# Score products of three attention layers on 64 rows instead of 32, with one operand masked, and a new order of TensorE's steps

## The chip, the core and the metric

The program runs on one core of a Trainium2 chip, in one launch. Its time is the device time in microseconds (us), the median of three runs. The engines are TensorE (PE; PEld is its weight load), VectorE (DVE), ScalarE (ACT), GpSimd (POOL) and SyncE (SP), which issues the DMAs.

## What is computed

Four residual attention layers follow each other on `x` of shape (2, 128, 32, 32), that is two batches of 128 channels and N = 1024 places.

```python
# layer 0: 4 heads of 4 channels; softmax over the query index n
q, k, v = (einsum('hdc,bcn->bhdn', W, xf) + b for W, b in ...)
A = softmax(einsum('bhdn,bhdm->bhnm', q, k), axis=-2)
x = gamma * (Wo @ einsum('bhdn,bhnm->bhdm', v, A) + bo) + x
# layer 1: one head, q and k of 16 channels, v of 128
x = x + gamma * (v @ softmax(q.T k, axis=2))
# layer 2: 8 heads of 16 channels; group norm; k and v from the 2x2-pooled x (256 places)
attn = softmax(einsum('bhdq,bhdk->bhqk', q, k) * scale, axis=-1)
x = x + wproj @ (attn v)
# layer 3: group norm, one head of 128 channels
x = x + out_w @ softmax(q k.T * scale) v + out_b
```

All data are float32; some products are made from values rounded to `fp32r`.

## The kernel before

**Tiles and steps.** The work is cut into steps, and `ORDER` is a string with one letter for each step, in the order in which TensorE issues them. Every other engine walks the same list (`plan`) and does its part of each step, so the string sets the order of all queues. The letters: `N` projections and norms (`k`, `q`, `stats`, `norm`), `V` value projections, `A` and `B` score tiles, `T` the transpose of the maxima (`top`), `P` the product of probabilities and values, `E` and `Y` outputs, denominators (`den`), their broadcast (`bcast`) and projections of the output.

**A unit of attention** (layer L, batch b, group g) goes: eight A tiles (L784 for layers 0 and 1, L789 for odd tiles of some, L797 for layer 2, L802 for layer 3) make rounded scores of 128 x 1024 in `products`; DVE reduces each to its maxima (`neg_max`, L604, L601, L607). A transpose (L815) and one ACT copy turn the maxima into rows (`max_rows`), and DMAs from SP (L388, L393, L397, L399) put them beside an operand as one more row, so that the second product comes out with the maximum already taken off. Then eight B tiles (L823 in layer 0, L828 in layer 1, L834 in layer 2, L838 and L844 in layer 3) make the scores again with that row, ACT takes the exponent (L495) into a ring of `NP` = 8 tiles `probs`, and P steps multiply with the values into `attn_acc` (L863: four products, each 32 columns wide, side by side, in layers 0 and 2; L869: 128 columns in layers 1 and 3).

**Rings.** `products` has three slots of 128 x 1024 (`RING`); a slot is free when DVE (A, N steps) or ACT (B steps) has read it. A unit of layer 1 or 3 has its exponents summed on POOL and DVE (L366).

**Rows.** In layers 0 to 2 a head's operands stand in one of four groups of 32 partitions (`GROUP`). A score tile is two products, each with 32 rows of contraction, on two neighbouring groups: a head pair in layers 0 and 2, two halves of the columns in layer 1. Layer 0 has head pair `g // 2`; in layers 1 and 2 the pair of groups changes from tile to tile. This is the core of it in layer 0:

```python
rows = slice(GROUP * (2 * (g // 2) + a), GROUP * (2 * (g // 2) + a) + GROUP)
tile = slice(HALF * mh + 128 * mt, HALF * mh + 128 * (mt + 1))
mm = nc.tensor.matmul(slot(s)[:, halves[a]], RA[b][rows, tile], RB[b][rows, halves[nh]],
                      start=True, stop=True)
```

**A start** has the projections of batch 0 (L756 and L760, first and second half), for which ACT makes the rounded part (L456, `stage_hi`) and DVE the rest (L570). `RA` (`rounded_a`) holds k and `RB` (`rounded_b`) q of layer 0. `wait_tile` waits until a tile is complete, `wait_read` until it has been read.

Of the kernel before, what the change touches and what calls it, by code (L numbers as in the profile page):

```python
# [20 lines left out]
F32 = mybir.dt.float32  # L21
# [14 lines left out]
GROUP = 32  # L36
ONE = 16
RING = 3
MAX_DMAS = {0: 2, 1: 4, 2: 4, 3: 1}
NP = 8  # L40
# [7 lines left out]
FIRST = [("w0k", 128), ("b0k", 1), ("s0k", 1), ("w0q", 128), ("b0q", 1), ("s0q", 1), ("w0v", 16), ("b0v", 16)]  # L48
REST = [("gam0", 4), ("gam0c", 1), ("b0o", 1), ("w0o", 128), ("ident", 128), ("pick0", 72), ("w1q", 128), ("w1k", 128), ("b1q", 1),
# [25 lines left out]
def groups(L, b):  # L75
# [12 lines left out]
    "NNAAAAAAANNAVATAAABABABAABVBAPTAABPAABBABAABPBABPT"  # L88
    "ABAPABAPBABPBABABAPTBPPABBPABBPBBAPBBAPAPABPBABBPT"
    "AAVPPPBAEAEBABEBABPNNVABABBPTAAAPPPABABABABABBPTBA"  # L90
    "BAPAPABPPBABPAPPBAPPAPBABPPAPBAPATPBPPAPABPAAPEPBB"
    "BEBBTNPBBNPPBPNBPBNNBBBBPBVPPAAPAAPAAAAEATEABEBBBA"
    "AANNAVABABBPTABAAPBABABAPBAPPABBPBBETPPPPEBEBYEPBE"
    "PPPNBNPPBPNNBPPAAPABPAPPBAPPAAEPAPEVNTNBNPNNBBPBAA"
    "PAVAAPAAPAPPATAAPPABABABABABPTBBBPBBBPBPPBBBPPBEPP"
    "PEEYEENBNBBNNBAAPAAPPAPAAAPVPTPPBBBPBEPBPBEPPPPPBP"
    "PBPPPPPPEPPE"
# [28 lines left out]
def build_plan():  # L126
# [17 lines left out]
    following = {c: iter(s) for c, s in steps.items()}  # L144
    return [next(following[c]) for c in ORDER]


def attention_layers(nc, x, first, rest, sel, out):
# [61 lines left out]
    with ExitStack() as ctx:  # L210
# [22 lines left out]
        KF2 = [sb(f"k2_rows{b}", [128, 2, NKV]) for b in range(B)]  # L233
        KR2 = [sb(f"k2_rounded{b}", [128, 2, NKV], F32R) for b in range(B)]
# [32 lines left out]

        ps = ctx.enter_context(nc.psum_tensor("products", [128, RING, N], F32))
# [4 lines left out]
        cleared = sem("cleared")  # L273
        consts_ready, consts_act = sem("consts_ready"), sem("consts_act")
# [5 lines left out]
        act_copy = sem("act_copy")  # L280
        max_folded = sem("max_folded")
# [70 lines left out]

        norm_no = number(("norm",))
# [17 lines left out]
        def _(sp):  # L371
# [6 lines left out]
            for s in plan:  # L378
                kind, L, b = s[0], s[1], s[2] if len(s) > 2 else None
                if kind == "top":  # L380
# [4 lines left out]
                    if L == 0:  # L385
                        for a in range(2):
                            row = GROUP * (2 * (g // 2) + a) + ONE
                            sp.dma_start(RA[b][row:row + 1, halves[g % 2]].bitcast(F32),  # L388
                                         ZR[4 * a:4 * a + 4, i, :]).then_inc(maxrows_in[b], 16)
                    elif L == 1:  # L390
                        for j in range(4):
                            row, h = GROUP * j + ONE, j % 2
                            sp.dma_start(FA[b][row:row + 1, halves[h]], ZR[4 * h:4 * h + 4, i, :]).then_inc(maxrows_in[b], 16)  # L393
                    elif L == 2:
                        for j in range(4):
# [29 lines left out]
        def _(act):  # L425
            for s in plan:
# [9 lines left out]
                elif kind in ("q", "k"):  # L436

                    if s not in full_no:
                        wait_tile(act, s)
                        wait_ops_free(act, L, b)  # L440
                        nc.scalar.activation(KR2[b][:, :, :].rearrange("p g n -> p (g n)"), slot(s)[:, 0:2 * NKV],
                                             ACT.Identity, bias=w("one2k")).then_inc(act_copy, 1)
                        continue
                    for h in halves:
# [18 lines left out]
                        hi.then_inc(act_copy if h.start else act_half, 1)  # L463
                elif kind == "v" and L > 0:
# [31 lines left out]
                elif kind == "out" and (L in (0, 2) or s[3] == 0):  # L496
# [8 lines left out]
                    h = halves[s[3] % 2] if L == 0 else slice(0, N)  # L505
                    nc.scalar.activation(O[o_tile[u]][:, h], acc[:, h], ACT.Identity).then_inc(acc_out, 1)  # L506
# [534 lines left out]
```

## Time and profile before

| | us (the clock: share) |
|---|---|
| median of 3 runs | 434.34 |
| lowest and highest | 433.93, 436.12 |
| the profiled execution | 433.25 |
| its span, first to last instruction | 431.2 |
| mean granted clock of TensorE in the span | 0.865 |

The profile is of one execution. Its span is 2.05 us shorter than that execution's own time, and that time is 1.09 us under the median. The profile names idle time by what ended it, and it gives TensorE's granted clock by stretch, where 1.00 stands for 2.4 GHz and 0.50 for 1.2 GHz; the first 10.8 us have no clock record, and the page shows them as if at 1.00. TensorE's busy time is modelled from starts, so that a lone product counts with its latency.

### The profile page before, as it was taken

What the parts mean: (1) busy time and instruction counts of PE and PEld (TensorE: products, weight loads), DVE (VectorE), ACT (ScalarE), POOL (GpSimd) and SP (SyncE); (2) the same over time, 40 slices, a digit from 0 to 9 for tenths busy, and PEclk for the clock granted to TensorE, in tenths of its full rate; (3) what the DMA queues carried; (4) which work ended last, traced back from release to release, by engine and by line L of the source; (5) the groups of instructions that cost most, each with busy time, mean ns of one, the idle gap of its engine ahead of it and who ended that gap; (6) DMA issues with size and microseconds to landing.
All of it is one profiled execution on the core that took longest, in us unless ns stands there. A gap on an engine that the chain in (4) does not pass through costs nothing.

```text
span 431.2 us, 4565 instructions
## 1 busy us (share of the span) xinstructions
PE 375.4 (87%) x1756; PEld 162.1 (38%) x1756; DVE 252.0 (58%) x312; ACT 187.2 (43%) x228; POOL 53.3 (12%) x36
## 2 busy tenths in 40 slices
PE   5689789999899989877998898987988997899994
PEld 2245222334223342333442342453444233364541
DVE  1876776775845575383666345695296016592733
ACT  3034478856533357902365534215404571513210
POOL 4000000000006400000000043200420000300820
PEclk9685699988869985976599998988995899999998
DMA  7000000000000000000000000000000000000011
GB/s 277 0 0 2 0 1 3 0 2 0 2 1 2 0 0 0 3 0 3 0 1 2 2 0 0 0 0 2 1 3 1 2 2 0 0 2 0 2 49 49
DMA packets 1508, 4.44 MB, mean 10 GB/s; under 512 B 352, under 2 KB 720, under 8 KB 1360
## 3 DMA queue, kind: packets, MB, share of 16 engines
q1 hardware_dynamic: 1488, 4.16, 2.6%
q8 instruction: 14, 0.23, 0.2%
q14 instruction: 6, 0.05, 0.0%
HBM read 2.99 MB, written 1.05 MB: 9 GB/s over the span
## 4 chain that ended last, share of the span: by engine, by line
PE 65%; DVE 19%; ACT 5%; issue 5%; DMA 3%; SPq 2%; ACTq 0%; DVEq 0%
PE attn_acc L869 12%; PE attn_acc L863 9%; DVE neg_max L604 7%; PE products L834 6%; PE products L756 5%; PE products L838 5%; PE products L760 4%; PE products L823 3%; PE products L828 3%; PE products L768 3%; PE products L784 3%; DVE neg_max L601 3%; ACT probs L495 3%; PE products L898 2%; DVE neg_max L607 2%
## 5 line engine op out<-in xcount | busy, mean ns | idle before, releaser
L495 ACT ACTIVATE probs<-products 128x1024 f32<-128x1024 f32 x128 | 127.1, 1023 | 111.5 <-PE products L828 32.0
L604 DVE TENSOR_REDUCE neg_max<-products 128x2 f32<-128x1024 f32 x64 | 76.2, 1220 | 32.6 <-PE products L784 28.3
L869 PE MATMUL attn_acc<-probs,v 128*128 128x512 f32 x128 | 64.0, 612 | 0.0
L863 PE MATMUL attn_acc<-probs,v 128*32 128x512 f32 x384 | 59.6, 713 | 0.0
L601 DVE TENSOR_REDUCE neg_max<-products 128x4 f32<-128x1024 f32 x32 | 37.4, 1217 | 19.4 <-PE products L797 19.3
L366 POOL TENSOR_TENSOR prob_sum<-prob_sum,probs 128x1024 f32<-128x1024 f32 x16 | 38.5, 2405 | 72.7 <-ACT probs L495 71.6
L366 POOL TENSOR_TENSOR prob_sum<-probs 128x1024 f32<-128x1024 f32 x4 | 9.4, 2356 | 286.2 <-ACT probs L495 262.0
L607 DVE TENSOR_REDUCE neg_max<-products 128x1 f32<-128x1024 f32 x32 | 37.4, 1218 | 11.7 <-PE products L789 4.9
L784 PE MATMUL products<-rounded_b,rounded_a 32*128 32x512 f32 x128 | 35.3, 567 | 9.4 <-DVE neg_max L604 5.7
L823 PE MATMUL products<-rounded_a,rounded_b 32*128 32x512 f32 x128 | 34.6, 566 | 7.4 <-DVE neg_max L604 1.9
L838 PE MATMUL products<-rows_a,rows_b 128*128 128x512 f32 x64 | 31.9, 623 | 0.0
L869 PEld LDWEIGHTS attn_acc<-probs,v 128*128 128x128 f32 x128 | 22.0, 189 | 21.9 <-issue 18.0
L622 DVE RECIPROCAL recips<-products 128x128 f32<-128x128 f32 x10 | 9.5, 954 | 33.4 <-PE products L889 33.4
L784 PEld LDWEIGHTS products<-rounded_b,rounded_a 32*128 32x128 f32 x128 | 13.4, 211 | 33.4 <-DVE neg_max L604 15.9
L823 PEld LDWEIGHTS products<-rounded_a,rounded_b 32*128 32x128 f32 x128 | 13.5, 215 | 28.8 <-DVE neg_max L604 11.3
L834 PE MATMUL products<-rows_a,k_rows 32*128 32x512 f32 x64 | 20.5, 938 | 3.9 <-DMA rows_a<-max_rows 3.9
L506 ACT ACTIVATE attn_out<-attn_acc 128x512 f32<-128x512 f32 (+1 forms) x16 | 13.0, 811 | 23.0 <-PE attn_acc L869 13.8
L756 PE MATMUL products<-x,w 128*128 128x512 f32 x16 | 14.8, 1028 | 5.1 <-DMA x<-x 4.8
L863 PEld LDWEIGHTS attn_acc<-probs,v 128*32 128x32 f32 x384 | 9.1, 118 | 22.2 <-issue 17.3
L838 PEld LDWEIGHTS products<-rows_a,rows_b 128*128 128x128 f32 x64 | 12.5, 198 | 13.0 <-issue 12.3
L828 PE MATMUL products<-rows_a,rows_b 32*128 32x512 f32 x64 | 16.3, 639 | 0.6 <-DMA rows_a<-max_rows 0.6
L844 PE MATMUL products<-max_rows,max_picker 128*128 128x512 f32 x32 | 16.8, 605 | 0.0
(124 smaller groups left out, 390.1 us busy)
## 6 DMA issues: line engine op xcount, KB each, us to landing
w<-w_rest SPq DMA_DIRECT2D x1, 1235.0 KB, 7.9
x<-x SPq DMA_DIRECT2D x2, 512.0 KB, 4.4
y<-x SPq DMA_DIRECT2D x2, 512.0 KB, 2.6
tmp<-row_selector SPq DMA_DIRECT2D x1, 512.0 KB, 8.7
rounded_a<-max_rows SPq DMA_DIRECT2D x16, 2.0 KB
w<-w_first SPq DMA_DIRECT2D x1, 146.0 KB, 2.2
rows_a<-max_rows SPq DMA_DIRECT2D x8, 2.0 KB
rows_a<-max_rows SPq DMA_DIRECT2D x8, 4.0 KB
```

The lines of the kernel that those rows point to most:

```text
L366: engine.tensor_tensor(DS[:, :], first_in, P[:, n % NP, :], ALU.add).then_inc(den_acc, 1)
L495: nc.scalar.activation(P[:, n % NP, :], slot(s), ACT.Exp, scale=SCALE[L]).then_inc(read_act, 1)
L601: nc.vector.tensor_reduce(out=m2, in_=slot(s).rearrange("p (a i k) -> p a i k", a=2, i=2), op=ALU.max, axis=AX.X, negate=True).then_inc(re ...
L604: nc.vector.tensor_reduce(out=m[:, 2 * t:2 * t + 2], in_=slot(s).rearrange("p (a n) -> p a n", a=2), op=ALU.max, axis=AX.X, negate=True).t ...
L607: nc.vector.tensor_reduce(out=m[:, t:t + 1], in_=slot(s), op=ALU.max, axis=AX.X, negate=True).then_inc(read_dve, 1)
L756: nc.tensor.matmul(slot(s)[:, halves[0]], wt, src[:, halves[0]], start=True, stop=True).then_inc(half_full, 1)
L784: mm = nc.tensor.matmul(slot(s)[:, halves[a]], RA[b][rows, tile], RB[b][rows, halves[nh]], start=True, stop=True)
L823: mm = nc.tensor.matmul(slot(s)[:, halves[a]], RB[b][rows, 128 * t:128 * (t + 1)], RA[b][rows, halves[g % 2]], start=True, stop=True)
L834: mm = nc.tensor.matmul(slot(s)[:, halves[a]], KF2[b][rows, g, 128 * kt:128 * (kt + 1)], (FA, FB)[g][b][rows, halves[half]], start=True, s ...
L838: nc.tensor.matmul(slot(s)[:, h], FB[b][:, 128 * t:128 * (t + 1)], FA[b][:, h], start=True, stop=False)
L863: mm = nc.tensor.matmul(acc[32 * j:32 * j + 32, h], lhs, P[:, b_no[q] % NP, halves[a]], start=t0 == 0 if L == 0 else t0 % 2 == 0, stop=t0 ...
L869: mm = nc.tensor.matmul(acc[:, h], V13[b][:, t0, :], P[:, b_no[q] % NP, h], start=t0 == first, stop=t0 == last)
```

## The change

**Rows.** A group of 64 partitions (`WIDE`) takes the place of the two groups of 32. A score tile is still two products of 512 columns (four of 256 in layer 2's A), but each now has 64 rows of contraction: rows 0 to 63 and rows 64 to 127. In layers 0 and 2 the 64 rows hold two heads, one of each head pair, in 32 rows each; one operand exists in two copies, and in each the rows of the other head pair are zero, so that only one head is summed. For layer 0 the copies of q are `Q0` (`q_even`, pair 0) and `RB` itself (pair 1), made by ACT from `RB` with a scale of 1 or 0 for each partition (`group_mask`). For layer 2 `KR2` and `KF2` get two copies, by a second ACT and a second DVE instruction. Layer 1 has its 17 rows in 64, the rest being zero in the weights. The weights on the host are packed to match.

**DMAs of the maxima.** One for each unit of layers 0 and 2 (two and four before), two for layer 1 (four before). A DMA of layer 0 for pair 1 waits until the B tiles of pair 0 are made, as both pairs now use the same partitions of `RA`.

**Start.** DVE clears a tile `zeros`, and TensorE runs five products of 256 columns with it (`WARMUP`) before its first step.

**Ring.** `NP` goes from 8 to 13 `probs` tiles.

**Order.** `ORDER` has the same 462 letters in another order (the letter `W`, for which the code is there, does not occur).

```diff
-NP = 8
+NP = 13
+WARMUP = 5
...
                     if L == 0:
-                        for a in range(2):
-                            row = GROUP * (2 * (g // 2) + a) + ONE
-                            sp.dma_start(RA[b][row:row + 1, halves[g % 2]].bitcast(F32),
-                                         ZR[4 * a:4 * a + 4, i, :]).then_inc(maxrows_in[b], 16)
+                        row = GROUP * (g // 2) + ONE
+                        if g >= 2:
+                            wait_tile(sp, ("B", 0, b, g - 2, 7))
+                        sp.dma_start(RA[b][row:row + WIDE + 1:WIDE, halves[g % 2]].bitcast(F32),
+                                     ZR[0:8, i, :]).then_inc(maxrows_in[b], 16)
...
                     elif L == 2:
-                        for j in range(4):
-                            row = GROUP * j + ONE
-                            sp.dma_start((FA, FB)[g][b][row:row + 1, :], ZR[8 * j:8 * j + 8, i, :]).then_inc(maxrows_in[b], 16)
+                        sp.dma_start((FA, FB)[g][b][ONE:ONE + 3 * GROUP + 1:GROUP, :],
+                                     ZR[0:32, i, :]).then_inc(maxrows_in[b], 16)
...
-                        nc.scalar.activation(KR2[b][:, :, :].rearrange("p g n -> p (g n)"), slot(s)[:, 0:2 * NKV],
-                                             ACT.Identity, bias=w("one2k")).then_inc(act_copy, 1)
+                        for p in range(2):
+                            masked = nc.scalar.activation(KR2[b][:, p, :, :].rearrange("p g n -> p (g n)"),
+                                                          slot(s)[:, 0:2 * NKV], ACT.Identity,
+                                                          scale=w("group_mask")[:, p:p + 1],
+                                                          bias=w("one2k")[:, p:p + 1])
+                        masked.then_inc(act_copy, 1)
...
+                    if (kind, L) == ("q", 0):
+                        wait_read(act, s)
+                        for p in range(2):
+                            nc.scalar.activation(q0_parity(b, p)[:, :], RB[b][:, :].bitcast(F32), ACT.Identity,
+                                                 scale=w("group_mask")[:, p:p + 1]).then_inc(q0_masked, 1)
...
+            pe.wait_ge(zeroed, 1)
+            for i in range(WARMUP):
+                nc.tensor.matmul(slot(jobs[0])[:, 0:NKV], zeros[:, 0:128], zeros[:, :], start=True, stop=True)
...
                     if t == 0:
-                        if L == 2:
+                        if L == 0:
+                            pe.wait_ge(q0_masked, 2 * q0_no[("q", 0, b)] + g // 2 + 1)
+                            if g >= 2:
+                                pe.wait_ge(maxrows_in[b], max_count(0, b, g - 2))
+                        elif L == 2:
...
                         for a in range(2):
-                            rows = slice(GROUP * (2 * (g // 2) + a), GROUP * (2 * (g // 2) + a) + GROUP)
+                            rows = slice(WIDE * a, WIDE * a + WIDE)
                             tile = slice(HALF * mh + 128 * mt, HALF * mh + 128 * (mt + 1))
-                            mm = nc.tensor.matmul(slot(s)[:, halves[a]], RA[b][rows, tile], RB[b][rows, halves[nh]],
+                            mm = nc.tensor.matmul(slot(s)[:, halves[a]], RA[b][rows, tile], q0_parity(b, g // 2)[rows, halves[nh]],
                                                   start=True, stop=True)
...
-                            rows = slice(GROUP * (2 * (t % 2) + i), GROUP * (2 * (t % 2) + i) + GROUP)
+                            rows = slice(WIDE * i, WIDE * i + WIDE)
...
-                                rows = slice(GROUP * (2 * hp + a), GROUP * (2 * hp + a) + GROUP)
+                                rows = slice(WIDE * a, WIDE * a + WIDE)
```

**The start on TensorE, before.** `x0` and `x1` are the batches' inputs; L756 and L760 are the projections of k and q by halves, L784 layer 0's A tiles (two products each), L768 the value projection. L756 and L760 stand twice for each batch (k, then q); the repeat is left out.

```order
L756 MATMUL products<-x0,w1 128x512
L760 MATMUL products<-x0,w1 128x512
...
L784 MATMUL products<-rounded_b0,rounded_a0 128x512 x14
L756 MATMUL products<-x1,w1 128x512
L760 MATMUL products<-x1,w1 128x512
...
L784 MATMUL products<-rounded_b0,rounded_a0 128x512 x2
L768 MATMUL products<-w1,x0 128x16 x8
```

**The same place now.** L759 are the products with zeros, L793 and L797 the projections, L805 the value projections, L825 the A tiles.

```order
L759 MATMUL products<-zeros 128x256 x5
L793 MATMUL products<-x0,w1 128x512
L797 MATMUL products<-x0,w1 128x512
...
L805 MATMUL products<-w1,x0 128x16 x8
L793 MATMUL products<-x1,w1 128x512
L797 MATMUL products<-x1,w1 128x512
...
L825 MATMUL products<-q0_even0,rounded_a0 128x512 x2
L805 MATMUL products<-w1,x1 128x16 x8
L825 MATMUL products<-q0_even0,rounded_a0 128x512 x16
```

Both batches' projections and both value projections now stand ahead of the second A tile; before, batch 1's stood among the A tiles of batch 0, and its value projection later still.

**ACT at the same place, now.** L474 is the rounded part of k and q, L485 the masked copies.

```order
L474 ACTIVATE stage_hi<-products,lo_bias_q,w1 128x512 x2
L485 ACTIVATE q0_even0<-rounded_b0,w1 128x1024
L485 ACTIVATE rounded_b0<-rounded_b0,w1 128x1024
L474 ACTIVATE stage_hi<-products,lo_bias_k,w1 128x512 x2
L474 ACTIVATE stage_hi<-products,lo_bias_q,w1 128x512 x2
L485 ACTIVATE q0_even1<-rounded_b1,w1 128x1024
```

The masked copies stand in ACT's queue between the two batches, and the first A tile waits for the first of them.

**SP's DMAs of layer 2's maxima,** batch 0, before (`rows_a0` is group 0, `rows_b0` group 1):

```order
L397 DMA rows_a0<-max_rows 1x8x128 [waits tile_read_act]
L397 DMA rows_a0<-max_rows 1x8x128 x3
L397 DMA rows_b0<-max_rows 1x8x128 [waits tile_read_act]
L397 DMA rows_b0<-max_rows 1x8x128 x3
```

and now:

```order
L410 DMA rows_a0<-max_rows 4x8x128 [waits tile_read_act]
L410 DMA rows_b0<-max_rows 4x8x128 [waits tile_read_act]
```

Four transfers of one row each have become one of four rows.

## Rows read from the trace of the kernel before

**Rows 1.** The page: span, busy PE, granted clock in 40 slices.

```profile
span 431.2 us, 4565 instructions
...
PE 375.4 (87%) x1756; PEld 162.1 (38%) x1756; DVE 252.0 (58%) x312; ACT 187.2 (43%) x228; POOL 53.3 (12%) x36
...
PEclk9685699988869985976599998988995899999998
```

**Rows 2.** The page: the chain that ended last, by engine.

```profile
PE 65%; DVE 19%; ACT 5%; issue 5%; DMA 3%; SPq 2%; ACTq 0%; DVEq 0%
```

**Rows 3.** Busy time by stretch: nine stretches of low clock, and their sum.

```profile
core 0: us, PE busy (x) PEld busy (x) DVE busy (x) ACT busy (x) POOL busy (x), PEclk, DMA share, GB/s
31.30:44.90 13.60, 12.50 (x51) 7.08 (x51) 8.66 (x10) 5.39 (x6) 0.00 (x0) 0.50 0.01 1
...
157.60:171.20 13.60, 12.93 (x55) 4.78 (x55) 8.27 (x28) 9.38 (x14) 0.00 (x0) 0.50 0.00 0
...
sum 92.20, PE 83.26 PEld 33.62 DVE 52.21 ACT 37.99 POOL 0.00; mean PE 9.25 PEld 3.74 DVE 5.80 ACT 4.22 POOL 0.00
```

**Rows 4.** Busy time by stretch: two of low clock, two of full clock.

```profile
31.30:41.50 10.20, 9.10 (x36) 6.09 (x36) 7.25 (x8) 4.10 (x4) 0.00 (x0) 0.50 0.01 2
55.20:65.50 10.30, 8.27 (x55) 2.84 (x53) 8.24 (x8) 8.17 (x10) 0.00 (x0) 1.00 0.00 0
60.00:80.00 20.00, 17.86 (x129) 5.31 (x121) 13.74 (x13) 16.80 (x20) 0.00 (x0) 1.00 0.01 1
...
324.80:335.10 10.30, 8.71 (x36) 4.58 (x36) 6.00 (x5) 4.37 (x5) 0.00 (x0) 0.50 0.00 0
```

**Rows 5.** L863 alone, by stretch: PE, PEld, clock, DMA.

```profile
31.30:41.50 10.20, 0.00 (x0) 0.00 (x0) 0.50 0.01 2
55.20:65.50 10.30, 3.20 (x24) 0.47 (x24) 1.00 0.00 0
```

**Rows 6.** PE's waits: who for whom, us in total, times, longest.

```profile
PE products L834 <- DMA rows_a<-max_rows: 3.9, 2, 2.7
PE products L924 <- ACT x_norm L520: 3.7, 2, 3.2
...
PE products L756 <- ACT x_norm L526: 3.6, 3, 1.8
```

**Rows 7.** The start in order of time: start, us, engine, line.

```profile
4.79 2.04 PE L756 MATMUL products<-x,w 128*128 128x512 f32 x2 [4.79 <-DMA x<-x]
6.62 1.91 PE L760 MATMUL products<-x,w 128*128 128x512 f32 x2
8.33 1.92 PE L756 MATMUL products<-x,w 128*128 128x512 f32 x2
...
27.24 1.21 DVE L604 TENSOR_REDUCE neg_max<-products 128x2 f32<-128x1024 f32 x1
```

**Rows 8.** Line 397, SP's DMAs of layer 2's maxima: duration ns min/median/max, first and last start.

```profile
L397 SPq DMA_DIRECT2D rows_a<-max_rows x8: 626/629/796, 196.4 to 323.8; - x8
```

**Rows 9.** One unit's DMAs of line 397 in order of time.

```profile
196.42 2.82 SPq L397 DMA_DIRECT2D rows_a<-max_rows  x4
```

**Rows 10.** Neighbouring score tiles in order of time: at low clock, then full.

```profile
51.50 0.79 PE L784 MATMUL products<-rounded_b,rounded_a 32*128 32x512 f32 x2 [0.60 <-DVE neg_max L604]
51.51 0.79 PE L823 MATMUL products<-rounded_a,rounded_b 32*128 32x512 f32 x2
...
58.26 0.50 PE L784 MATMUL products<-rounded_b,rounded_a 32*128 32x512 f32 x2 [0.70 <-DVE neg_max L604]
58.54 0.50 PE L823 MATMUL products<-rounded_a,rounded_b 32*128 32x512 f32 x2
```

**Rows 11.** Groups of instructions by line: busy us, mean ns, idle before.

```profile
L604 DVE TENSOR_REDUCE neg_max<-products 128x2 f32<-128x1024 f32 x64 | 76.2, 1220 | 32.6 <-PE products L784 28.3 <-PE products L823 2.6 <-PE products L828 1.7
...
L570 DVE SCALAR_TENSOR_TENSOR rounded_a<-products,w,stage_hi 128x512 fp32r<-128x512 f32 x4 | 3.0, 751 | 7.1 <-ACT stage_hi L456 7.1
...
L511 ACT ACTIVATE tmp<-products 128x1024 f32<-128x1024 f32 x2 | 2.0, 1024 | 10.2 <-PE products L907 10.2
```

More of the change, by code:

```diff
@@ L144, in build_plan @@
     following = {c: iter(s) for c, s in steps.items()}
+    following["W"] = (("warm", i) for i in range(len(ORDER)))
     return [next(following[c]) for c in ORDER]
@@ L232, in attention_layers @@
         RB = [sb(f"rounded_b{b}", [128, N], F32R) for b in range(B)]
-        KF2 = [sb(f"k2_rows{b}", [128, 2, NKV]) for b in range(B)]
-        KR2 = [sb(f"k2_rounded{b}", [128, 2, NKV], F32R) for b in range(B)]
+        Q0 = [sb(f"q0_even{b}", [128, N], F32R) for b in range(B)]
+        KF2 = [sb(f"k2_rows{b}", [128, 2, 2, NKV]) for b in range(B)]
+        KR2 = [sb(f"k2_rounded{b}", [128, 2, 2, NKV], F32R) for b in range(B)]
         M3 = [sb(f"max3_rows{b}", [128, N], F32R) for b in range(B)]
@@ L266, in attention_layers @@
         eps = sb("eps", [C, 2])
+        zeros = sb("zeros", [128, NKV])
         ps = ctx.enter_context(nc.psum_tensor("products", [128, RING, N], F32))
@@ L351, in x_upd_before, with q0_parity @@
             return len([p for p in plan[:plan.index(s)] if p[0] == "bcast" and p[1] != 2])
+        q0_no = {s: n for n, s in enumerate([s for s in split0 if s[0] == "q"])}
+        def q0_parity(b, p):
+            return (Q0, RB)[p][b]
         norm_no = number(("norm",))
@@ L504, in _ @@
                         wait_read(act, last)
-                    h = halves[s[3] % 2] if L == 0 else slice(0, N)
-                    nc.scalar.activation(O[o_tile[u]][:, h], acc[:, h], ACT.Identity).then_inc(acc_out, 1)
+                    h, bank = (halves[s[3] % 2], halves[s[3] % 2]) if L == 0 else (slice(0, N), slice(0, N))
+                    nc.scalar.activation(O[o_tile[u]][:, h], acc[:, bank], ACT.Identity).then_inc(acc_out, 1)
                 elif kind == "y" and L == 0:
@@ L537, in link @@
                 dve.wait_ge(dve_chain, links[0])
+            nc.vector.memset(zeros[:, :], 0.0).then_inc(zeroed, 1)
             nc.vector.memset(eps[:, 0:1], EPS)
@@ L557, in _ @@
                         dve.wait_ge(act_copy, half_no[s] + 1)
-                        nc.vector.tensor_scalar(KF2[b][:, :, :].rearrange("p g n -> p (g n)"), slot(s)[:, 0:2 * NKV],
-                                                w("one2k"), None, ALU.add).then_inc(read_dve, 1)
+                        for p in range(2):
+                            masked = nc.vector.tensor_scalar(KF2[b][:, p, :, :].rearrange("p g n -> p (g n)"),
+                                                             slot(s)[:, 0:2 * NKV], w("group_mask")[:, p:p + 1],
+                                                             w("one2k")[:, p:p + 1], ALU.mult, ALU.add)
+                        masked.then_inc(read_dve, 1)
                         continue
@@ L727, in full @@
                 mm.then_inc(tile_full, 1)
+            pe.wait_ge(zeroed, 1)
+            for i in range(WARMUP):
+                nc.tensor.matmul(slot(jobs[0])[:, 0:NKV], zeros[:, 0:128], zeros[:, :], start=True, stop=True)
             for s in plan:
                 kind, L, b = s[0], s[1], s[2] if len(s) > 2 else None
+                if kind == "warm":
+                    following = next(p for p in plan[plan.index(s):] if p in job)
+                    if job[following] >= RING:
+                        wait_read(pe, jobs[job[following] - RING])
+                    nc.tensor.matmul(slot(following)[:, 0:NKV], zeros[:, 0:128], zeros[:, :], start=True, stop=True)
+                    continue
                 if kind == "ya":
@@ L832, in _ @@
                         for a in range(2):
[L833 to L834 removed]
+                            rows = slice(WIDE * a, WIDE * a + WIDE)
+                            mm = nc.tensor.matmul(slot(s)[:, halves[a]], KF2[b][rows, hp, g, 128 * kt:128 * (kt + 1)],
                                                   (FA, FB)[g][b][rows, halves[half]], start=True, stop=True)
@@ L950, in rows0 @@
     def rows0(m, ones):
-        z = np.zeros((H0, GROUP, m.shape[-1]), np.float32)
-        z[:, 0:4 * D0] = np.tile(m.reshape(H0, D0, -1), (1, 4, 1))
+        z = np.zeros((2, 2, GROUP, m.shape[-1]), np.float32)
+        z[:, :, 0:4 * D0] = np.tile(m.reshape(2, 2, D0, -1).swapaxes(0, 1), (1, 1, 4, 1))
         if ones:
-            z[:, ONE] = 1
+            z[:, :, ONE] = 1
         return z.reshape(128, -1)
     def rows1(m, ones):
-        z = np.zeros((4, GROUP, m.shape[-1]), np.float32)
+        z = np.zeros((2, WIDE, m.shape[-1]), np.float32)
         z[:, 0:D1] = m
@@ L965, in rows2 @@
     def rows2(m):
-        z = np.zeros((H2, GROUP, C), np.float32)
-        z[:, 0:D2] = m.reshape(H2, D2, C)
+        z = np.zeros((2, 2, 2, GROUP, C), np.float32)
+        z[:, :, :, 0:D2] = m.reshape(2, 2, 2, D2, C).swapaxes(1, 2)
         return z.reshape(2 * 128, C)
@@ L972 @@
     s0q[:, D0:2 * D0] = s0q[:, 3 * D0:4 * D0] = -1
-    one2k = np.zeros((4, GROUP, 1), np.float32)
-    one2k[:, ONE] = 1
+    group_mask = np.zeros((2, 2, GROUP, 2), np.float32)
+    one2k = np.zeros((2, 2, GROUP, 2), np.float32)
+    for p in range(2):
+        group_mask[:, p, :, p] = 1
+        one2k[:, p, ONE, p] = 1
     w0o = np.zeros((4, 32, 2, 2, 32), np.float32)
```

49 lines of the change are left out of this document (26 added, 23 removed), and 2 rows, old and new, of the table REST.

## The prediction

> **What bounds the kernel now.** I read the page first: TensorE is busy 87% of the span, DVE 58%, ACT 43%, and the clock line falls to 5 to 8 tenths in many slices of the first four fifths and stays at 8 or 9 after [rows 1]. Then the chain that ended last: 65% of it is PE, 19% DVE [rows 2]. So the end is set by TensorE, with DVE next, and part of TensorE's time is work at half clock.
>
> Next I cut the span where the granted clock changes. Nine stretches of layers 0 to 2, 92.2 us together, ran at 0.50, that is at 1.2 GHz; PE was busy 83.3 us of them, DVE 52.2, ACT 38.0 [rows 3]. (A tenth, in which batch 1 is projected at the start, I price with the start; a few short ones lie in norms, where PE had nothing to do.) The question is what TensorE did there. From 31.3 to 41.5 us it was busy 9.10 of 10.2 us and the clock was 0.50; from 55.2 to 65.5 us it was busy 8.27 of 10.3 us, less, and the clock was 1.00 [rows 4]. The score products with 32 rows are in both. What differs is that the second stretch has 24 products of the probabilities (L863, 128 rows, four side by side) and the first has none [rows 5]. The stretch from 324.8 to 335.1 us is like the first: B and A tiles of layer 2 on 32 rows, 8.71 of 10.3 us busy, clock 0.50 [rows 4]. So in this kernel the low clock goes with stretches in which little of the array is in use, not with stretches in which PE is idle. That the clock follows the width of the products is my reading of these rows; nothing in them proves it.
>
> **The change part by part**, against the profiled execution's 433.3 us (1.1 under the median).
>
> *Rows of the score products, the clock.* 64 rows in place of 32 cost no product more: the count and the columns are the same. If the clock follows the part of the array in use, every score product of layers 0 to 2 now counts double, and the stretches of rows 3 come near the fuller ones. Their bounds: nothing (the clock is as before), and the other end from the busiest engine. At full clock PE's 83.3 us would be about half, 42, so DVE's 52.2 us is next; in the stretch from 157.6 us ACT's 9.4 stands above DVE's 8.3, which makes 53.3 us. No engine reaches 100%: in the best full-clock stretch of layer 0, from 60 to 80 us, the busier of ACT and DVE was at 16.8 of 20 us, 0.84 [rows 4]. 53.3 / 0.84 = 63.5, and 92.2 - 63.5 = 28.7 us. I take -26: nearer to the upper end, since 64 rows double exactly what fills these stretches, less something for the stretch from 157.6 us, where a broadcast and a norm stand in line.
>
> *The start.* Before, PE's first product waits until 4.79 us for `x`, and a pair of half-products takes 1.71 us (6.62 to 8.33), which is the low clock [rows 7]; the clock rises at 10.8 us. The five products with zeros have half the columns each, 5 x 0.855 = 4.3 us at that pace; they start at about 1 us and end at about 5.3, so they hold the projections up by 0.5 us, and the clock may rise up to 3.8 us earlier. That leaves some 6 of the 8 half-products of batch 0 at 0.43 instead of 0.855 us: about 2 us less. In turn the masked copy of q (ACT, 1.02 us by the nearest copy of 128 x 1024 [rows 11]) stands before the first A tile, and the second one, 1.0 us more, delays batch 1's copies on ACT; these and DVE's four pieces of 0.75 us [rows 11] now come before the run of maxima. I get: q complete at 11, masked twice by 13.1, batch 1's rounded parts to 16.2, its rest to 16.9, then eight reductions of 1.22 us [rows 11] without a break, to 26.7 us. Before, the eighth ran from 27.24 to 28.45 us [rows 7]. Sum -2 (between +1, if the clock does not rise early, and -4).
>
> *DMAs.* SP needs 0.63 us to issue one of layer 2's [rows 8], and four in a row, one unit's, took 2.82 us from the first issue to the end of the last [rows 9]; PE's first B product waits for the last to land. PE waited 3.9 us in two places for these rows [rows 6]. With one issue the row is there some 1.9 us earlier in each unit of layer 2 (3 x 0.63), 1.3 in layer 1. Four units of layer 2 and two of layer 1 have it, but the time is only won where PE waited: -3 (0 to -6). One DMA of four rows may land later than one of one row; it would have to take 1.9 us more to undo this. The new wait of SP in layer 0, on the last B tile of pair 0, stands ahead of nothing that is due: SP's next DMA is the next unit's.
>
> *Overlap between tiles.* With 32 rows, neighbours on different row groups ran at the same time: at 51.50 and 51.51 us two tiles begin together and both last 0.79 us, while two tiles on the same group at full clock begin 0.28 us apart, at 58.26 and 58.54 [rows 10]. With 64 rows every tile takes both halves, and no two can. The trace has 36 such neighbours, the first at 40.98, the last at 342.36 us. At 0.28 us that is 10 us of TensorE at most; where PE waited for DVE afterwards it costs nothing. I take +5 (0 to +10).
>
> *The skill against this edit.* The Trainium skill, page "TensorE: Matmul & The Clock Gate", part "Packing small matmuls — row/col tiling", says that products with few rows gain by lying on distinct groups of 32 rows, so that several run at once. The rows just named agree with it. By it, with all 224 score tiles of layers 0 to 2 two and two at once, half of them hidden, the edit would give away 112 x 0.28 = 31 us, not 5; the kernel before had 36 of them so, which is why I keep to the count.
>
> *Second copies of k in layer 2.* One more DVE instruction of 128 x 512 (0.75 us, as in rows 11) after one more on ACT, for two batches: +1.5, as PE waits there for both.
>
> *The order.* Most of it I can't price. Two places I can: the norms. PE waited 3.7 us for L924 and 3.6 us for the projections after a norm [rows 6]. The new order puts more work into the holes of two of the four norms: two B steps after `stats` of layer 2, batch 1, where none stood, and two B and two P steps between `norm` and `q` of layer 3, batch 0. That is 2 to 4 us of work in each. I take -5 (+4 to -8: it could as well open holes elsewhere). The 13 probability tiles I take at nothing: ACT's exponents wait for products, not for a free tile.
>
> Sum: 433.3 - 26 - 2 - 3 + 5 + 1.5 - 5 = 403.8. **Forecast 404 us.**
>
> **The rivals.**
>
> *A: the clock rises, and DVE and ACT hold the time.* The nine stretches shrink by half of what I take, 13 us, as the order makes PE wait for the reductions and exponents that it used to hide. For it: DVE and PE stand in the chain together, 19% and 65% [rows 2], and L604's idle time before a reduction is 32.6 us over 64 [rows 11], so the slack is not large. Against: DVE's whole busy time is 58% of the span. 403.8 + 13 = 417 us.
>
> *B: the change does not do what it says, the clock stays.* Then -26 is 0, and -2 for the start is 0: 403.8 + 28 = 432. For it: zero rows may not count, and the low clock may come from short waits between tiles, which are in these stretches too. Against: rows 4, where the busier stretch has the lower clock. The Trainium skill speaks for this rival: on the same page, "What's actually happening", the clock is said to follow how busy the PE is, with no word of rows; by it, 64 rows would change nothing. Rows 4 and 5 disagree with the plain form of that rule.
>
> *C: slower.* The overlap is lost where it is dear, and the clock stays low. At 0.50 two tiles that ran together now need a tile time each; that is about twice 0.28, 0.56 us, and 36 x 0.56 = 20 us instead of 5. 432 + 15 = 447. It decides as soon as the clock term is under some 13 us with most of the neighbours on the chain; below that the sum is over 433. Against: it needs both.
>
> *D: all goes well.* Clock -29, order -12, no overlap on the chain: 433.3 - 29 - 3 - 4 + 0 + 1.5 - 12 = 387.
>
> **How the numbers follow.** Forecast (392 to 412): 0.60. A (412 to 425): 0.18. B (428 to 437): 0.09. C: 0.05. D (under 392): 0.08. The range that leaves out no more than 2 in 10, with the ends of the unknown costs in it, is 388 to 425: it holds the forecast's case, A and the nearer half of D, 0.82. A measurement of this kernel tells about 0.5%, 2.2 us, from no change. Faster than 432.2: forecast, A, D and near half of B, 0.90. Same: half of B, 0.04. Slower: C and a piece of B, 0.06.
>
> **What would show it.** Right: the clock line of the page at 9 or above in most slices of layers 0 to 2, the span's mean clock over 0.93; stretches with only score tiles at 1.00; PE busy under 350 us; DVE's share over 62%. The start: the first reduction at about 16 to 17 us, the eighth ended by 27. The DMAs: no wait of PE for rows of layer 2 over 1 us. The overlap: no two score tiles that begin together. Wrong: a clock line as before with 64-row tiles in it (B); a clock near 1 and a time over 415, with PE waiting for `neg_max` (A). The forecast as a whole falls if the 32-row stretches were slow for another reason than the rows, which is its main step.

## The result: 390.25 us after 434.13

The changed kernel takes 390.25 us (median of 4 runs, 388.21 to 392.45); the kernel before, on the same chip, 434.13 (433.59 to 436.12). The ratio is 0.898, 95% interval 0.891 to 0.906: faster. That is 13.8 us under the forecast of 404: inside the stated range of 388 to 425, but under the forecast's own band of 392 to 412, where rival D stood. The profiled execution of after took 388.21 us, with a span of 386.2. The times of some kernels below fall in two groups, over 1.5% apart, the upper one at a lower granted clock; such kernels are compared by the lower group, and the traces are of the lower group unless the text says otherwise.

Lines move by the new code; the score tiles are L825, L830, L838 (A of layers 0, 1, 2) and L864, L869, L875 (B), the probability products L904 and L910, the reductions L632, L635, L629, the layer 2 DMA L410. The page of after, beside [rows 1, 2]:

```profile
span 386.2 us, 4574 instructions
...
PE 348.5 (90%) x1766; PEld 157.3 (41%) x1766; DVE 255.8 (66%) x315; ACT 191.8 (50%) x234; POOL 52.4 (14%) x36
...
PEclk9955999999999999999999999998999998999998
...
PE 71%; DVE 18%; ACT 6%; issue 4%; DVEq 0%; ACTq 0%
```

PE's busy time fell by 27 us, its idle time from 55.8 to 37.7, and the low clock is gone but for slices 3 and 4 (18.7 to 39.2 us) and three short pieces, two at waits for a norm and one at the end, which show as 8. DVE and ACT have nearly the work they had, and a larger share of a shorter span. The start in order of time, DVE alone:

```profile
16.27 1.22 DVE L632 TENSOR_REDUCE neg_max<-products 128x2 f32<-128x1024 f32 x1
17.40 0.28 DVE L610 TENSOR_TENSOR v<-products,w 128x128 f32<-128x128 f32 x1
17.60 8.00 DVE L632 TENSOR_REDUCE neg_max<-products 128x2 f32<-128x1024 f32 x7
```

The first reduction starts at 16.27 and the eighth has ended at 25.6 us; before, at 28.45 [rows 7]. PE's waits, beside [rows 6]:

```profile
PE products L793 <- ACT x_norm L550: 8.9, 4, 2.7
PE products L864 <- DVE neg_max L632: 2.8, 5, 0.8
...
PE products L965 <- ACT x_norm L544: 1.5, 1, 1.5
```

The 3.9 us for the rows of layer 2 are gone. The waits at the norms (L793 and L965) are not: 10.4 us together, where the answering ones were 7.3.

### The profile page after: what moved, and what is told of

It reads as the page before. It is cut to its first block, busy times and chain, and to the rows that moved or that the text cites. A ratio compares the mean times of both kernels' runs of the same rounds, so it can differ in the third digit from the quotient of the medians.

```text
span 386.2 us, 4574 instructions
## 1 busy us (share of the span) xinstructions
PE 348.5 (90%) x1766; PEld 157.3 (41%) x1766; DVE 255.8 (66%) x315; ACT 191.8 (50%) x234; POOL 52.4 (14%) x36
## 4 chain that ended last, share of the span: by engine, by line
PE 71%; DVE 18%; ACT 6%; issue 4%; DVEq 0%; ACTq 0%
PE attn_acc L910 13%; PE attn_acc L904 11%; PE products L875 8%; DVE neg_max L632 5%; PE products L879 5%; PE products L825 4%; PE products L864 4%; PE products L793 3%; PE products L869 3%; PE products L797 3%; PE products L838 2%; PE products L939 2%; PE products L805 2%; ACT probs L518 2%; DVE neg_max L635 2%
## 5 line engine op out<-in xcount | busy, mean ns | idle before, releaser
L632 DVE TENSOR_REDUCE neg_max<-products 128x2 f32<-128x1024 f32 x64 | 75.7, 1219 | 17.6 <-PE products L825 17.6
L910 PE MATMUL attn_acc<-probs,v 128*128 128x512 f32 x128 | 62.7, 607 | 0.0
L904 PE MATMUL attn_acc<-probs,v 128*32 128x512 f32 x384 | 51.1, 612 | 0.4 <-ACT probs L518 0.4
L635 DVE TENSOR_REDUCE neg_max<-products 128x1 f32<-128x1024 f32 x32 | 37.9, 1220 | 5.7 <-PE products L830 3.7
L629 DVE TENSOR_REDUCE neg_max<-products 128x4 f32<-128x1024 f32 x32 | 37.5, 1217 | 4.5 <-PE products L838 4.4
L910 PEld LDWEIGHTS attn_acc<-probs,v 128*128 128x128 f32 x128 | 22.4, 189 | 21.3 <-issue 18.8
L879 PE MATMUL products<-rows_a,rows_b 128*128 128x512 f32 x64 | 30.5, 599 | 0.6 <-ACT probs L518 0.5
L825 PE MATMUL products<-q_even,rounded_a 64*128 64x512 f32 x64 | 17.7, 569 | 3.8 <-DVE neg_max L632 2.6
L864 PE MATMUL products<-rounded_a,q_even 64*128 64x512 f32 x64 | 16.3, 520 | 2.5 <-DVE neg_max L632 1.4
L793 PE MATMUL products<-x_norm,w 128*128 128x512 f32 x16 | 10.3, 729 | 8.9 <-ACT x_norm L550 8.9
L825 PE MATMUL products<-rounded_b,rounded_a 64*128 64x512 f32 x64 | 17.1, 535 | 0.7 <-ACT probs L518 0.5
L380 DVE TENSOR_TENSOR prob_sum<-prob_sum,probs 128x1024 f32<-128x1024 f32 x8 | 9.8, 1221 | 11.2 <-POOL prob_sum L380 6.9
L879 PEld LDWEIGHTS products<-rows_a,rows_b 128*128 128x128 f32 x64 | 11.8, 189 | 12.4 <-issue 10.7
L875 PE MATMUL products<-rows_a,k_rows 64*128 64x512 f32 x64 | 16.3, 612 | 0.5 <-DVE neg_max L629 0.4
L869 PE MATMUL products<-rows_a,rows_b 64*128 64x512 f32 x64 | 15.9, 606 | 0.0
L864 PE MATMUL products<-rounded_a,rounded_b 64*128 64x512 f32 x64 | 14.1, 458 | 1.9 <-DVE neg_max L632 1.4
```

The costliest lines, as they stand in the source:

```text
L380: engine.tensor_tensor(DS[:, :], first_in, P[:, n % NP, :], ALU.add).then_inc(den_acc, 1)
L629: nc.vector.tensor_reduce(out=m2, in_=slot(s).rearrange("p (a i k) -> p a i k", a=2, i=2), op=ALU.max, axis=AX.X, negate=True).then_inc(re ...
L632: nc.vector.tensor_reduce(out=m[:, 2 * t:2 * t + 2], in_=slot(s).rearrange("p (a n) -> p a n", a=2), op=ALU.max, axis=AX.X, negate=True).t ...
L635: nc.vector.tensor_reduce(out=m[:, t:t + 1], in_=slot(s), op=ALU.max, axis=AX.X, negate=True).then_inc(read_dve, 1)
L864: mm = nc.tensor.matmul(slot(s)[:, halves[a]], q0_parity(b, g // 2)[rows, 128 * t:128 * (t + 1)], RA[b][rows, halves[g % 2]], start=True, ...
L869: mm = nc.tensor.matmul(slot(s)[:, h], FB[b][rows, 128 * t:128 * (t + 1)], FA[b][rows, h], start=True, stop=True)
```

## The experiments

The theory was the prediction's: the 64 rows give the clock back, and that is most of the gain. The rival was that the order does it. So each part was undone alone, then both, then smaller parts. The kernel before, timed again beside the experiments, took 433.4, 435.6 and 433.0 us; ratios are always to the kernel before on the same chip. Differences between kernels of different experiments carry that shift of 1 to 3 us besides their own spread.

Two reckonings are used below. *Low clock* is the time that the span holds at 0.50: twice one minus the mean clock, times the span. *Work at full clock* is PE's busy time with the part that fell into low clock counted half; the change of a span is then the change of PE's idle time, plus that of this work, plus half the change of the time in which PE was busy at low clock. This last time is read from the windows of each trace's low stretches, added up.

**1. The rows undone, order kept.**

```diff
-rows = slice(WIDE * i, WIDE * i + WIDE)
+rows = slice(WIDE * i, WIDE * i + GROUP)
```

(and so in all score products of layers 0 to 2: only the 32 rows that are not zero.)

> The changed kernel, but each score product of layers 0 to 2 takes only the 32 rows that are not zero, with the same results, masks, DMAs and order. Theory 'rows set the clock': the granted clock falls back to about 0.87 to 0.90 and low stretches stand in layers 0 to 2 again; the time rises by 20 to 30 us, to 410 to 420. Rival 'the order (and the deeper ring) keeps TensorE fed, the rows count for nothing': the clock stays near 0.96 and the time within 2 us of 390, or a few us less, as head pairs on distinct rows can overlap again.

Four times: 389.84, 391.46, 403.49, 403.85. The pair once more, both on one chip:

> The changed kernel with the score products of layers 0 to 2 on the 32 rows that are not zero, once more: its four times before were 389.8, 391.5, 403.5 and 403.9 us, the changed kernel's 388.2 to 392.5. If the rows still matter under the new order, its median stands 5 to 10 us above the changed kernel's on the same chip, at a clock lower by 0.02 or more. If they don't, within 2 us.

> The changed kernel itself, unaltered, so that the kernels of this call have it on the same chip. Of the kernels timed so far on other chips the one with the maxima in separate DMAs took 399.0 us and the one with zeros between the first tiles 396.6. If the chips differ by that much, the changed kernel takes 396 to 399 us here; if those edits cost what their times say, it takes 388 to 393 us.

The 32-row kernel took 389.8, 391.0, 391.7, 403.7, 405.0 and 408.1 us, the changed kernel on that chip 389.9 (387.9 to 392.5; 0.902 [0.897, 0.907]), as before, so the chips don't differ here. Five of the 32-row kernel's ten times are 389.8 to 391.7, at a mean clock of 0.931 to 0.939, and five are 403.5 to 408.1, at 0.883 to 0.904. The ratio of the lower three on the changed kernel's chip is 0.904 [0.899, 0.908]: in the lower five the 64 rows are worth about 1 us, which can't be told from nothing. (By the medians of all six it is 7.8 us.) The theory's 410 to 420 us came in none of the ten; the rival's time came in the lower five, though not its clock of 0.96. What made the other five longer isn't shown, as there is no trace of them; the changed kernel's ten had 0.949 to 0.962 and none over 392.5 us.

The traces say why so little is left. These are the low stretches added up, 32 rows and then 64, both under the new order:

```profile
sum 46.92, PE 39.67 PEld 14.97 DVE 26.68 ACT 17.03 POOL 1.96; mean PE 4.96 PEld 1.87 DVE 3.33 ACT 2.13 POOL 0.24
```

```profile
sum 29.60, PE 23.01 PEld 9.06 DVE 20.29 ACT 9.83 POOL 1.99; mean PE 5.75 PEld 2.27 DVE 5.07 ACT 2.46 POOL 0.50
```

PE is busy 348.5 us in both. With 64 rows 16.7 us less of that is at low clock, which is worth 8.3; the work at full clock is 8.3 us more (337.0 after 328.7), since tiles overlap less. The two cancel.

**2. The order undone, rows kept.** `ORDER` as it was.

> The changed kernel with the order of before. Theory 'rows set the clock': the clock is near 0.95 and the time 395 to 405, so 30 us or more of the 44 come without the new order. Rival 'the order': 415 or more, with a clock under 0.92.

413.06 us (412.51 to 415.61), ratio 0.955 [0.951, 0.959], clock 0.938: the time is 2 us short of the rival's 415, the clock near the theory's 0.95. The order is worth 23 us with 64 rows. The prediction gave it 5.

**3. Both undone.**

> The changed kernel with both of its parts undone at once: score products of layers 0 to 2 on the 32 rows that are not zero, and the order of the steps of the kernel before; what stays is the single DMA a unit for the maxima, two probability tiles fewer or more, the zeros at the start and the code around them. It is the fourth corner of a square whose other three stand at 434 (kernel before, 32 rows and old order), 413 (64 rows and old order) and 397.5 (32 rows and new order). Theory, that the 64 rows give the clock where the order is old: 428 to 434 us, clock 0.87 to 0.89, so that the rows are worth 15 to 20 us under the old order and 3 to 8 under the new. Rival, that what the 64-row kernel with the old order gained came from the DMAs, the zeros and the start: 412 to 418 us.

Median 424.94 (422.99 to 435.09; without the one long time 424.4), ratio 0.976 [0.968, 0.985], clock 0.884: between the two theories. By this corner the 64 rows are worth 12 us under the old order (9 by the ratios), and 9 to 11 us belong to neither rows nor order. Clock lines of the two kernels with the old order, 32 rows and then 64:

```profile
PEclk9685689987658996778899999998998899999998
```

```profile
PEclk9585899999899998987999999988999999999998
```

and their low stretches added up, in the same order:

```profile
sum 98.62, PE 89.11 PEld 32.16 DVE 54.29 ACT 38.41 POOL 0.00; mean PE 7.43 PEld 2.68 DVE 4.52 ACT 3.20 POOL 0.00
```

```profile
sum 50.89, PE 42.91 PEld 18.80 DVE 36.16 ACT 16.33 POOL 0.00; mean PE 4.77 PEld 2.09 DVE 4.02 ACT 1.81 POOL 0.00
```

The rows did what they were expected to do: with nothing else changed, the time at low clock fell from 98 to 51 us of the span, and PE's busy time in it by 46.2, which is worth 23.1. But the span fell by 12.9 us only (423.4 to 410.5). The rest can be followed: PE's idle time fell by 1.5 us, and its work at full clock rose by 11.7, from 330.4 to 342.1. That is the lost overlap. The kernels have the same products; the traces give one score product 0.59 us at full clock in both (at 322.38 us with 32 rows, at 122.37 with 64); and by line the 11.7 us stand at the score tiles, the largest part, 5.4 us, at L875, layer 2's B tiles. Tiles that begin within 0.06 us of each other are 28 pairs with 32 rows and 10 with 64.

**4. The DMAs of the maxima.** In the changed kernel, as before:

```diff
-sp.dma_start((FA, FB)[g][b][ONE:ONE + 3 * GROUP + 1:GROUP, :], ZR[0:32, i, :])
+for j in range(4):
+    row = GROUP * j + ONE
+    sp.dma_start((FA, FB)[g][b][row:row + 1, :], ZR[8 * j:8 * j + 8, i, :])
```

(layer 0 likewise with two in place of one)

> The changed kernel with the maxima of a unit moved in four DMAs (layer 2) and two (layer 0) in place of one, as they were before. Theory by the prediction's term of 3 us for these DMAs: 392 to 394 us. Rival, that the transfers lie beside other work: within 1 us of the changed kernel's 390.3 us.

398.95 us (395.21 to 400.22), 0.915 [0.906, 0.924]: 9 us slower than the changed kernel, past both expectations. And with 32 rows and the old order:

> 32 rows, the old order, and the maxima in separate DMAs as before: of the change only the zeros at the start, the 13 probability tiles and the code around them are left. With one DMA a unit the same kernel took 424.9 us, beside 435.6 of the kernel before. Theory, that the DMAs made that difference, as they make the one between the changed kernel (390) and its version with separate DMAs (399): 432 to 436 us. Rival, that the start and the tiles made it: 424 to 428 us.

438.01 us (437.36 to 438.44), ratio 1.013 [1.008, 1.017]; without the split 424.94. The DMAs make 13 us there, 2 us past the theory's end. The term was 3, bounded at 6. PE's waits of the changed kernel with split DMAs:

```profile
PE products L877 <- DMA rows_a<-max_rows: 3.4, 2, 1.8
...
PE products L877 <- DMA rows_b<-max_rows: 1.5, 2, 1.0
...
PE products L866 <- DMA rounded_a<-max_rows: 1.0, 1, 1.0
```

and its clock line:

```profile
PEclk9955999899999999999999889998989999899998
```

This trace is of that kernel's longest execution, 400.22 us, beside the changed kernel's shortest. PE waited 5.9 us for those DMAs (0.3 in the changed kernel); its other waits of 1 us and more are those of the changed kernel within 0.1 us. So of the 12.0 us between the spans, 5.4 are idle time. The other 6.6 are PE's busy time at low clock, 36.1 us in place of 23.0, halved; the work at full clock is 337.0 in both. In the old order the same edit makes 12.2 us of span: 5.1 of idle time, 10.3 of clock (109.8 us busy at low clock in place of 89.1), less 3.3 of work. So about half or more of what the DMAs cost is clock. That each wait brings its own low clock is not shown: of the four short low stretches that the split adds in the new order, one begins at such a wait (293.7 us), and those at 68.4, 222.0 and 235.6 don't. The changed kernel's own ten executions differ by as much as 10 us of low clock (from a mean of 0.962 over 386 us to 0.949 over 390).

Since 438.0 is 4 to 5 us above the kernel before, what is then left of the change (zeros, 13 tiles, masked copies of q and k, pairs on shared rows) costs that much under the old order; which of them, stays open but for two:

**5. The zeros at the start, and the probability tiles.** `WARMUP = 0`, and `NP = 8`.

> The changed kernel without the five products with zeros ahead of the first step. Theory (they bring the first rise of the clock some 3.5 us forward, though their data are zero): 2 to 3 us slower, 392 to 393, the projections of batch 0 at 0.85 us for a half-product instead of 0.43. Rival (masks and batch 1's projections stand behind anyway): within 0.7 us of 390.

> The changed kernel with 8 tiles of probabilities instead of 13. Theory (ACT waits for products, not for tiles): within 1 us of 390. Rival (the new order runs the exponents further ahead of their use and needs the room): 3 us or more slower, with ACT's exponents waiting for L910 or L904.

390.82 us (388.38 to 393.29) and 391.93 (388.12 to 392.67), ratios 0.902 and 0.905: no difference that can be told from the changed kernel in either. The zeros do raise the clock early. The first projections with them, then without:

```profile
5.34 1.02 PE L793 MATMUL products<-x,w 128*128 128x512 f32 x2
```

```profile
4.56 2.04 PE L793 MATMUL products<-x,w 128*128 128x512 f32 x2 [4.56 <-DMA x<-x]
```

But none of it is left at the end.

**6. Where in the list the order's gain is.** The list has the same steps handed out after 119 letters in both orders, and after 248. Old order, but letters 120 to 248 new (the first 40 of each):

```diff
-NNVABABBPTAAAPPPABABABABABBPTBABAPAPABPP
+BBAANNBTPAAVAABAPBAPPABAPBTBABPABBPABAPA
```

> 64 rows, and the order of the kernel before except for letters 120 to 248 of the list (from the middle of layer 1 of the first batch to layer 2 of that batch), which are those of the new order. The two lists have handed out the same steps at both joints. Theory, that the new order's gain of 23 us lies in that middle third, where the kernel with the old order waits for reductions at 154.6 to 194.9 us (PE 32.62 of 40.30): 396 to 402 us. Rival, that the gain is spread evenly over the list: 405 to 409 us.

402.66 us (401.29 to 403.45), 0.926 [0.919, 0.933]: 10 to 12 of the 23 us, just above the theory's 396 to 402. And letters 1 to 119 new:

> 64 rows, the new order for the first 119 letters of the list (to the middle of layer 1 of the first batch) and the old one from there on. With the old order throughout the kernel took 413 us, with the new one for letters 120 to 248 alone 403, with the new one throughout 390. Theory, that first and last parts share the remaining 12 us evenly: 406 to 408 us. Rival, that the gain of the order lies in the middle and the end, and the start gives nothing: 411 to 414 us. Third, that the start carries all the rest: 400 to 403 us.

412.69 us (409.12 to 414.11), 0.951 [0.945, 0.958]: as the rival had it, nothing that can be told from 413. By difference some 12 us are left to the last 214 letters, as far as parts add. The stretch from the end of layer 0 of batch 0 to the end of layer 2 of batch 0, by windows (the first is layer 1 of batch 0); old order, then the changed kernel:

```profile
92.10:154.60 62.50, 57.71 (x267) 21.90 (x267) 41.98 (x41) 31.95 (x37) 11.75 (x5) 0.97 0.00 1
154.60:238.60 84.00, 75.51 (x457) 31.71 (x458) 51.34 (x73) 45.77 (x59) 3.19 (x2) 0.94 0.01 1
```

```profile
87.00:141.50 54.50, 52.41 (x262) 21.78 (x266) 41.20 (x41) 31.28 (x38) 11.76 (x5) 1.00 0.00 1
141.50:219.20 77.70, 70.14 (x457) 30.50 (x451) 54.66 (x73) 43.73 (x56) 4.68 (x2) 1.00 0.01 2
```

146.5 us have become 132.2, with the same products. In both, PE is the busy engine; of the 14.3 us, PE is busy 10.7 less and idle 3.6 less; the old order has 13.6 us of low clock in there and the new one none, and half of that is 6.8; the other 3.9 of the busy time stay unexplained. DVE's waits in the part where that kernel has the new letters show what moved. Old order, from 92.1 to 194.9 us:

```profile
DVE neg_max L632 <- PE products L825: 16.4, 15, 2.4
DVE neg_max L629 <- PE products L838: 7.4, 2, 5.2
```

The changed kernel, from 87.0 to 171.9:

```profile
DVE neg_max L632 <- PE products L825: 8.7, 9, 2.0
...
DVE neg_max L629 <- PE products L838: 1.2, 2, 0.8
```

The kernel with the new order in the middle has 9.6 and 1.2 there. The letters fit that: `AANN`, two A tiles ahead of a norm, and `AAVAABAP` after it, in place of a run of one kind. Over the whole kernel DVE's waits for A tiles of layers 0 and 2 fell from 47.3 (old order) to 22.0 us. No run moves these letters alone, so that the A tiles are what wins the time is a reading. From the old order to the new one the span fell by 24.3 us: 9.2 of PE's idle time, 10.0 of clock (42.9 to 23.0 us busy at low clock, halved) and 5.1 of work at full clock, which stay unexplained.

**7. Zeros between the first score tiles.** In the changed kernel the clock is at half from 18.7 to 39.2 us. Eighteen products with zeros (`W`; the expectation says 19), of 256 columns each, were set between the tiles there.

```diff
-NNVNNAVAAAAAAAATAAABABABABAABAPT
+NNVNNAVAWAWAWAWAWAWAWAWTAWAWAWBAWBAWBAWBAWABAWPT
```

> The changed kernel with 19 products on zeros set between the first tiles of scores, at 17 to 40 us, where its clock is at half for 20.5 us (from 18.7 us on) and TensorE waits for the first reductions. Theory, that the zeros keep the clock there but VectorE sets the pace: 0 to 2 us gained, clock 1.00 there. Rival, that TensorE sets the pace: 4 to 6 us gained. Third, that the products stand in the way of the tiles: up to 3 us slower.

Median 396.59 us (396.52 to 404.43), 0.912 [0.905, 0.920], some 6 us slower; the third case by kind, and twice its size. Three of the four times are 396.5 to 396.6, at a clock of 0.971, above the changed kernel's 0.949 to 0.962: that is 23 us of low clock in place of 29 or more. So the 6 us are not clock; that the zeros stand in the tiles' way fits, but there is no trace of these three. The only trace is of the execution of 404.43 us, at 0.943, and nothing is read from it here.

**The traces side by side.** Span and PE busy are from the pages; PE idle, low clock and, in the last column, work at full clock are worked out as above (for the kernel before the clock of the first 10.8 us is missing, so it has none).

| kernel | median | span | PE busy | PE idle | low clock | work |
|---|---|---|---|---|---|---|
| before | 434.1 | 431.2 | 375.4 | 55.8 | 116 | |
| 32 rows, old order, split DMAs | 438.0 | 435.6 | 382.1 | 53.5 | 119 | 327.2 |
| 32 rows, old order | 424.9 | 423.4 | 375.0 | 48.4 | 98 | 330.4 |
| 64 rows, old order | 413.1 | 410.5 | 363.6 | 46.9 | 51 | 342.1 |
| 64 rows, new order in the middle | 402.7 | 399.4 | 356.0 | 43.4 | 38 | 340.6 |
| 32 rows, new order (lower five) | 391.0 | 387.7 | 348.5 | 39.2 | 47 | 328.7 |
| 64 rows, new order, split DMAs | 399.0 | 398.2 | 355.1 | 43.1 | 43 | 337.0 |
| after | 390.3 | 386.2 | 348.5 | 37.7 | 29 | 337.0 |

## Why the prediction was right, and where its sum was not

The sign, the kind of mechanism (PE's clock and PE's waits) and the range held. The single terms did not: two were too small by 10 and 18 us and two too large by 9 and 5. They erred in both directions, and that the sum of a wrong -21 and a wrong -5 stayed in the range is partly luck; the result lies where D was given 0.08. Going from before to after one step at a time, in this one order (another order of steps would divide the sum otherwise, and under the new order the rows come out at about 1 us):

| step | predicted | measured |
|---|---|---|
| start, tiles, second copies, pairs | -0.5 | +4 to +5 |
| DMAs | -3 | -13 |
| rows: clock and overlap | -26 + 5 = -21 | -12 |
| order | -5 | -23 |
| all | -29.5 | -44 |

*Rows and clock.* The reading of [rows 4, 5], that 64 rows raise the clock, is confirmed by two pairs of kernels that differ in nothing else (old order 98 to 51 us of low clock, new order 47 to 29). Its size, 26, is close to the 23.1 measured under the old order. What failed is the overlap: +5 was taken from 36 neighbours at 0.28 us, with half of them off the chain, where 11.7 us of work came back. That is above the upper end of that term, 10, and much of it is in layer 2's B tiles.

*DMAs.* The place was right, and the sign named for it came true: no wait of PE for rows of layer 2 is left. The step that failed is the sentence that "the time is only won where PE waited". Idle time is 5.4 and 5.1 us of what the split costs, near the upper bound of 6; the rest, 6.6 and 10.3 us of clock, had no term.

*The order.* This is the step that was mis-sized most, -5 with a bound of -8, for a measured 23. The price was put on holes at the norms, and there PE's waits grew, from 7.3 us before (8.4 with 64 rows and the old order) to 10.4. The gain is 9.2 us of idle time elsewhere, 10.0 of clock and 5.1 of work. It goes with a place that the prediction had before it and priced only in rival A as a danger: L604's 32.6 us of idle time before reductions [rows 11]. I said of the order that most of it couldn't be priced, and then gave it a bound of 8 us all the same; the idle time of PE and DVE at the A tiles would have been a wider and better one.

*The start.* First reduction and eighth came where they were forecast (16.27; 25.6). The masked copies took 1.15 us each. But taking the zeros out changed nothing.

*The probability tiles* at nothing: right, as far as 1.7 us can be told.

*The signs.* Clock line at 9 or above in most slices: yes. Mean clock over 0.93: 0.962. PE busy under 350: 348.5. DVE over 62%: 66%. No two score tiles that begin together: no, six pairs in layer 1 of batch 0 still begin 0.03 us apart (the first at 109.33 us). Stretches with only score tiles at 1.00: no; from 18.7 us until the first probability products at 36.52 PE had score tiles of 64 rows and one transpose, and ran at 0.50. Of the rivals, D (387) was nearest, but its clock of -29 and its overlap of 0 both failed. B is refuted by experiment 3. The step from 64 rows to the clock alone would not have carried the forecast: with it and the old order the kernel stands at 413, near A's number and 9 us over the forecast.

## What to carry to other kernels

When an edit makes or closes a hole on a busy TensorE, price the hole at its length and keep a second bound for the clock: here a wait of 5 us went with another 6.6 to 10.3 us of clock. Padding rows to raise the clock gives away overlap, and the two are to be weighed together: here 23.1 against 11.7 us under one order, 8.3 against 8.3 under another. An order of steps is to be bounded by the idle time it could remove on the engine that sets the end and on the one that feeds it, here DVE's waits for A tiles, rather than by the two or three places where a hole is seen. When several edits are made for one reason, take them off one by one and then two together: here the edit that the change is named for gave 12 of the 44 us under the old order, and about 1 us under the new one.

## What the runs showed of the hardware

**Busy time alone does not tell the clock.** The changed kernel, by windows:

```profile
18.70:28.70 10.00, 6.45 (x19) 2.56 (x19) 9.81 (x11) 0.27 (x1) 0.00 (x0) 0.50 0.00 0
28.70:39.20 10.50, 9.74 (x33) 3.65 (x35) 9.02 (x9) 5.38 (x6) 0.00 (x0) 0.50 0.01 2
39.20:52.40 13.20, 11.22 (x73) 3.81 (x69) 10.82 (x10) 10.50 (x12) 0.00 (x0) 1.00 0.00 1
```

PE is busy 93% of the second window at 0.50, and 85% of the third at 1.00 (at half clock the same products keep it busy longer). In four traces this low stretch ends 2 to 6 us after the first probability products of the kernel: those start at 36.52 (after), 41.70 (before), 40.10 (64 rows, old order) and 36.30 us (32 rows, new order), and the clock rises at 39.2, 44.9, 42.1 and 42.1. They have 128 rows. They are not the only work ahead of a rise: in the kernel before the clock rises at 24.5 us too, in the middle of batch 1's projections. What in the products counts wasn't tried apart from the rows.

The Trainium skill, page "TensorE: Matmul & The Clock Gate", part "What's actually happening", says that the clock is set by how busy PE has been. These windows don't agree with the plain form of it, and no more does experiment 3, where the same products on twice the rows halved the time at low clock.

**Zeros can raise the clock.** Five products with zeros ahead of the program's first step brought the first projections to full clock (1.02 us a pair in place of 2.04, experiment 5). Whether zeros can hold it between score tiles stays open: with them the whole kernel had 23 us of low clock in place of 29 or more, and took 6 us more (experiment 7).
